# Attention without TensorE transposes: probabilities turned in 32x32 squares on VectorE, gathered inside SBUF by transfers, three of eight key blocks in native float32

## The reference, cut to what matters

```python
x = x + attention(layernorm(x), ctx, ctx, gamma)   # 8 heads, scale 1/sqrt(128), on (B, 1024, 1024)
x = x + mixture(layernorm(x))
# attention: qh = q.reshape(B, 8, 128, L), kh = vh = ctx.reshape(B, 8, 128, L), L = 1024
qk  = einsum('bhdq,bhdl->bhql', qh, kh) * scale
ret = einsum('bhql,bhdl->bhdq', softmax(qk), vh)   # times gamma
# mixture: alpha = softmax(relu(x W1 + b1) W2 + b2); out = sum_k alpha_k U_k (V_k x), 8 experts of rank 64
```

## Time and profile before

| what | value |
|---|---|
| median of three runs | 1776.61 us |
| span of the profiled execution (first to last instruction) | 1775.2 us |
| granted TensorE clock | 1.00 of full speed throughout |
| PE busy | 98% of the span |
| DVE, ACT, POOL busy | 64%, 44%, 27% |
| data moved | 159.98 MB |

### The profile page before, as it was taken

The page is one execution under the profiler, slowest core; times in us unless marked ns, Lnnn a source line. Parts: engine busy times, 40 slices in busy tenths (PEclk is TensorE's granted clock), DMA queues, the critical chain, the costliest instruction groups (busy, mean ns, idle before and its releaser), DMA issues.

```text
span 1775.2 us, 25213 instructions
## 1 busy us (share of the span) xinstructions
PE 1739.8 (98%) x8736; PEld 1394.5 (79%) x8736; DVE 1137.6 (64%) x1608; ACT 774.0 (44%) x1314; POOL 473.1 (27%) x297
## 2 busy tenths in 40 slices
PE   7999999999999999999999999999999999999999
PEld 5778787878787877878787778787877878787877
DVE  7888888898888888888889743232423333232312
ACT  5666666666666666666666431212122121212120
POOL 4444445353544444444534200000000000000000
PEclk9999999999999999999999999999999999999999
DMA  4632323332334333333333403121121203021202
GB/s 149 220 102 95 113 86 110 93 118 95 118 95 118 95 112 101 95 115 88 109 93 106 160 1 107 36 95 47 65 77 37 105 0 138 4 101 40 95 0 72
DMA packets 73389, 159.98 MB, mean 90 GB/s; under 512 B 17552, under 2 KB 17552, under 8 KB 73360
## 3 DMA queue, kind: packets, MB, share of 16 engines
q1 hardware_dynamic: 73360, 159.59, 28.1%
...
...
## 4 chain that ended last, share of the span: by engine, by line
PE 85%; DVE 11%; issue 2%; ACT 1%; DMA 0%; DVEq 0%; POOL 0%
PE scores L850 20%; PE attended L429 16%; PE scores L396 15%; PE scores L893 10%; PE turned L410 10%; PE turned L911 5%; PE attended L911 5%; DVE q L507 4%; DVE pt_lo L486 3%; PE scores L930 2%; DVE neg_max L477 2%; DVE scaled L527 2%; ACT pt_hi L343 1%; PE turned L865 1%; PE turned L868 1%
## 5 line engine op out<-in xcount | busy, mean ns | idle before, releaser
L343 ACT ACTIVATE pt_hi<-turned 128x512 fp32r<-128x512 f32 x512 | 304.7, 595 | 314.9 <-PE turned L410 314.9
L410 PE MATMUL turned<-ident,probs 128*128 128x128 f32 x2048 | 388.9, 272 | 3.3 <-ACT probs L348 2.6
L410 PEld LDWEIGHTS turned<-ident,probs 128*128 128x128 f32 x2048 | 282.7, 140 | 100.8 <-ACT probs L348 19.4
L477 DVE TENSOR_REDUCE neg_max<-scores 128x1 f32<-128x1024 f32 x256 | 312.2, 1219 | 72.5 <-PE scores L396 67.6
L486 DVE TENSOR_TENSOR pt_lo<-turned,pt_hi 128x512 fp32r<-128x512 f32 x512 | 328.9, 683 | 30.9 <-ACT pt_hi L343 20.3
L348 ACT ACTIVATE probs<-scores,neg_max 128x1024 f32<-128x1024 f32 x256 | 285.9, 1117 | 48.0 <-DVE neg_max L477 47.9
L429 PE MATMUL attended<-pt_hi,v_hi 128*128 128x512 f32 x512 | 243.9, 476 | 18.8 <-DVE scaled L527 18.8
L429 PE MATMUL attended<-pt_hi,v_lo 128*128 128x512 f32 x512 | 223.6, 437 | 0.0
L429 PE MATMUL attended<-pt_lo,v_hi 128*128 128x512 f32 x512 | 223.2, 436 | 0.0
L988 DVE TENSOR_TENSOR ht_lo<-hidden,ht_hi 128x512 fp32r<-128x512 f32 x64 | 44.3, 693 | 258.6 <-ACT ht_hi L797 258.6
L850 PE MATMUL scores<-nt_hi,w_hi 128*128 128x512 f32 x512 | 200.0, 391 | 0.0
...
## 6 DMA issues: line engine op xcount, KB each, us to landing
...
```

What stands on the lines that cost most here:

```text
L343: nc.scalar.activation(pt_hi[half][:, 4 * part:4 * part + 4, col:col + P], src[:], ACT.Copy).then_inc(s_hi, 1)
L410: ins = pe.transpose(dst[:, i % 4, :], probs[j % 2][:, i * P:(i + 1) * P], ident[:])
L477: nc.vector.tensor_reduce(neg_max[:, j:j + 1], scores[j % 2][:], AX_X, ALU.max, negate=True).then_inc(s_max, 1)
```

## The change

The probabilities are no longer transposed on TensorE. For each query block DVE turns `probs` (128x1024) in squares of 32x32 into `pb` (`blocks`), which puts each square in place but leaves squares in the wrong partitions. When the four blocks of a half are turned, SP issues 16 transfers from SBUF to SBUF (`gather`), each from 32 partitions to 32 partitions, 8 key blocks by 128 columns, 128 KB in runs of 512 B; together they fill `pt`, keys on partitions, 2 MB. ACT copies key blocks 0 to 4 into high parts (`hi`), POOL subtracts the low parts; key blocks 5 to 7 are not split: they are multiplied once, in float32, with values `v_nat` loaded as they are. The last steps of a head come ten blocks behind its scores (`LAG`). There are now two PSUM banks `attended`.

Work moves between engines: the query scaling goes from DVE to ACT (as scale and shift), the gains from DVE to ACT, the high parts of keys and values from POOL to ACT, the low parts of the probabilities from DVE to POOL. The weights W1 and V, whose place in SBUF `pb` and the first `hi` now use, are loaded behind the last gathers instead of in the first heads; the first chunk is split by ACT and DVE. The mixture's products and loop stay the same, with other PSUM banks.

```diff
...
+    SPLIT = 5
+    NAT = JB - SPLIT
+    QB = 4
+    SB = P // QB
+    LAG = 10
+    QUARTER_KEYS = ((0, 1), (1, 2), (2, 3), (3, 5))
...
-    pt_hi, pt_lo = [], []
-    for b in range(2):
-        pt_hi.append(place.tensor(f"pt_hi{b}", [P, JB, BANK], F32R))
-        pt_lo.append(place.tensor(f"pt_lo{b}", [P, JB, BANK], F32R))
+    place = SbufMap(nc, shared["loaded_at"])
+    pb = [place.tensor(f"pb{b}", [P, QB * JB, HALF, SB]) for b in range(2)]
+    hi = [[place.tensor(f"pt_hi{b}_{q}", [P, hi_k - lo_k, BANK], F32R) for q, (lo_k, hi_k) in
+           enumerate(QUARTER_KEYS)] for b in range(1)]
+    top = SbufMap(nc, shared["top_at"])
+    x1_out = [top.tensor(f"x1_out{b}", [P, BANK]) for b in range(2)]
+    hi.append([(top if q < 2 else place).tensor(f"pt_hi1_{q}", [P, hi_k - lo_k, BANK], F32R)
+               for q, (lo_k, hi_k) in enumerate(QUARTER_KEYS)])
+    assert place.at == shared["loaded_end"]
+    pt, pt_lo = [], []
+    for b in range(4):
+        under = SbufMap(nc, place.at)
+        pt.append(place.tensor(f"pt{b}", [P, JB, BANK]))
+        pt_lo.append(under.tensor(f"pt_lo{b}", [P, JB, BANK], F32R))
...
+    v_hi = [place.tensor(f"v_hi{b}", [P, SPLIT, P], F32R) for b in range(2)]
+    v_lo = [place.tensor(f"v_lo{b}", [P, SPLIT, P], F32R) for b in range(2)]
+    v_nat = [place.tensor(f"v_nat{b}", [P, NAT, P]) for b in range(2)]
...
+    def quarter_in(h, n, j, parity, lag):
+        back = (j - lag) // JB
+        at = (j - lag) % JB
+        if isinstance(h, int) and h + back < 0 or isinstance(h, int) and h + back >= heads:
+            return None
+        return n + (j - lag), at // 4, at % 4, h + back, (parity + back) % 2
...
+            sp.dma_start(v_raw[:, 0:SPLIT, :], ctx_t[rows_of(h), 0:SPLIT * P].rearrange("p (b d) -> p b d", d=P)
+                         ).then_inc(s_v_in, 16)
+        def load_v_native(h, parity):
+            sp.dma_start(v_nat[parity][:], ctx_t[rows_of(h), SPLIT * P:].rearrange("p (b d) -> p b d", d=P)
+                         ).then_inc(s_vn_in, 16)
...
+        def gather(h, n, half, parity):
+            sp.wait_ge(s_blocks, n + 4 * half + 4)
+            dst = pt[2 * parity + half]
+            for a in range(QB):
+                for g in range(QB):
+                    sp.dma_start(dst[SB * g:SB * g + SB, :, P * a:P * a + P],
+                                 pb[half][SB * a:SB * a + SB, g::QB, :, :].rearrange("p k j c -> p k (j c)")
+                                 ).then_inc(s_gather[half], 16)
+        def send_gain(h, half):
+            sp.wait_ge(s_gain, h * 2 + half + 1)
+            sp.dma_start(scratch[bass.ds(h * 2 + half, 1), :].rearrange("a (p j) -> (a p) j", p=P),
+                         gain[half][:]).then_inc(s_gain_out, 16)
+        def spread_gain(h, half):
+            sp.wait_ge(s_gain_out, (h * 2 + half) * 16 + 16)
...
+            known = isinstance(h, int)
+            more = not (known and h + 2 >= heads)
+            if not first:
+                gather(h - 1, n - JB, 1, 1 - parity)
+                send_gain(h - 1, 0)
+            if not (known and h < 2):
+                store_x1(h - 2, 0)
             if last:
                 load_first(n)
+            if more:
+                sp.wait_ge(s_klo, h + 2)
+                load_k(h + 2)
             if not first:
+                spread_gain(h - 1, 0)
+            if not (known and h < 2):
+                sp.wait_ge(s_pv, n - JB)
+            load_v_native(h, parity)
             if not last:
+                sp.wait_ge(s_vlo, h + 1)
                 load_v(h + 1)
             if not first:
+                send_gain(h - 1, 1)
+            if not (known and h < 2):
+                store_x1(h - 2, 1)
+            if not first:
+                load_residual(h - 1)
+                spread_gain(h - 1, 1)
+            gather(h, n, 0, parity)
             if more:
                 sp.wait_ge(s_q32, h + 2)
                 load_x(h + 2)
...
+        gather(h - 1, n - JB, 1, 1)
+        sp.wait_ge(s_gather[0], heads * GATHERS)
+        for tile, dram in shared["w1_low_loads"]:
+            sp.dma_start(tile, dram).then_inc(shared["s_w1_low"], 16)
+        send_gain(h - 1, 0)
+        store_x1(h - 2, 0)
+        spread_gain(h - 1, 0)
+        sp.wait_ge(s_gather[1], heads * GATHERS)
+        for k, (tile, dram) in enumerate(shared["w1_high_loads"]):
+            sp.dma_start(tile, dram).then_inc(shared["s_w1_high"][k], 16)
+        send_gain(h - 1, 1)
+        store_x1(h - 2, 1)
+        load_residual(h - 1)
+        spread_gain(h - 1, 1)
+        sp.wait_ge(s_pv, n)
+        for tile, dram in shared["v_loads"]:
+            sp.dma_start(tile, dram).then_inc(shared["s_v_all"], 16)
...
+        def low_keys(h, b):
+            pool.wait_ge(s_khi, h + 1)
+            nc.gpsimd.tensor_tensor(k_lo[b][:], k_raw[:], as_f32(k_hi[b][:]), ALU.subtract).then_inc(s_klo, 1)
+        def low_values(h, b):
+            pool.wait_ge(s_vhi, h + 1)
+            nc.gpsimd.tensor_tensor(v_lo[b][:], v_raw[:, 0:SPLIT, :], as_f32(v_hi[b][:]), ALU.subtract).then_inc(s_vlo, 1)
...
+        def low_probs(quarter):
+            if quarter is None:
+                return
+            count, half, q, _, parity = quarter
+            keys = slice(*QUARTER_KEYS[q])
+            pool.wait_ge(s_pthi, count + 1)
+            nc.gpsimd.tensor_tensor(pt_lo[2 * parity + half][:, keys, :], pt[2 * parity + half][:, keys, :],
+                                    as_f32(hi[half][q][:]), ALU.subtract).then_inc(s_ptlo, 1)
...
+            early = isinstance(h, int) and h < 2
+            for j in range(JB):
+                low_probs(quarter_in(h, n, j, parity, LAG - 1))
+                if j == 1 and not last:
+                    low_keys(h + 1, 1 - parity)
+                if j == 3:
+                    low_values(h, parity)
+                    if not early:
+                        add_residual(h - 2, 1)
+                if j == 4 and not last:
+                    scale_of_queries(h + 1, 1 - parity)
+                if j == 6 and not last:
+                    low_queries(h + 1, 1 - parity)
+                if j == 7 and not first:
+                    add_residual(h - 1, 0)
+                if last and j in (4, 6):
+                    first_factor(j // 2 - 2)
...
-        def high_probs(t, j, n, part, early):
-            s_turn, s_hi = (s_turn0, s_hi0) if part == 0 else (s_turn1, s_hi1)
-            half = j // HALF
-            act.wait_ge(s_turn, t + 1)
-            if j % HALF == 0 and not early:
-                act.wait_ge(s_pv, n - JB + 4 * half + (2 if part == 0 else 4))
-            src = turned0 if part == 0 else turned1[j % 2]
-            col = j % HALF * P
-            nc.scalar.activation(pt_hi[half][:, 4 * part:4 * part + 4, col:col + P], src[:],
-                                 ACT.Copy).then_inc(s_hi, 1)
+        def high_probs(quarter):
+            if quarter is None:
+                return
+            count, half, q, head, parity = quarter
+            if q == 0:
+                act.wait_ge(s_gather[half], head * GATHERS + GATHERS)
+            if not (isinstance(head, int) and head < 1):
+                act.wait_ge(s_pv, count - (JB - 1))
+            nc.scalar.activation(hi[half][q][:], pt[2 * parity + half][:, slice(*QUARTER_KEYS[q]), :],
+                                 ACT.Copy).then_inc(s_pthi, 1)
         def exps(s, j, b):
             act.wait_ge(s_max, s + 1)
+            if not (isinstance(s, int) and s < 2):
+                act.wait_ge(s_blocks, s - 1)
             nc.scalar.activation(probs[j % 2][:], scores[j % 2][:], ACT.Exp, bias=neg_max[:, j:j + 1],
                                  accum_out=row_sum[b][:, j:j + 1]).then_inc(s_exp, 1)
+        def queries(h, b):
+            act.wait_ge(s_qshift, h + 1)
+            if not (isinstance(h, int) and h == 0):
+                act.wait_ge(s_qlo, h)
+            nc.scalar.activation(q32[:], x_raw[:], ACT.Identity, bias=q_shift[b][:],
+                                 scale=q_scale[b][:]).then_inc(s_q32, 1)
...
+        def high_keys(h, n, b):
+            act.wait_ge(s_k_in, h * 16 + 16)
+            if not (isinstance(h, int) and h < 2):
+                act.wait_ge(s_scores, n - JB)
+            nc.scalar.activation(k_hi[b][:], k_raw[:], ACT.Copy).then_inc(s_khi, 1)
+        def high_values(h, n, b):
+            act.wait_ge(s_v_in, h * 16 + 16)
+            if not (isinstance(h, int) and h < 2):
+                act.wait_ge(s_pv, n - JB)
+            nc.scalar.activation(v_hi[b][:], v_raw[:, 0:SPLIT, :], ACT.Copy).then_inc(s_vhi, 1)
...
             for j in range(JB):
-                back = (n + j - 1, (j - 1) % JB, n if j else n - JB)
-                early = first or (j == 0 and isinstance(h, int) and h == 1)
-                if not (first and j == 0):
-                    high_probs(*back, 0, early)
                 exps(n + j, j, parity)
-                if not (first and j == 0):
-                    high_probs(*back, 1, early)
```

(85 more changed lines are left out.)

361 lines of the change are left out of this document (123 added, 238 removed).

## The result

The changed kernel takes 1882.27 us (median of four runs, 1880.05 to 1884.17) against 1776.85 (1776.59 to 1777.53): the ratio is 1.0592, 95% interval 1.0577 to 1.0607. It is slower by 5.9%, above the forecast of 1650 and above its range.

What follows compares the result with a forecast made beforehand. It took DVE (25.0 us a head), transfers (25), PE (23.2) and POOL (22.6) as likeliest bounds, giving 26.2 a head: 5.5 + 838 + 22 + 782.8 = 1648 of span, forecast 1650 us, range 1605 to 1830.

Steps and rivals of the forecast that it cites:

- SP, the step that failed: SP's queue in each head: 43 issues at 0.43 us, 18.5 us, upper end 29.7.
- Transfers, 25 a head: Transfer engines in each head: old transfers 10.3 us plus gathers 15, total 25; upper end 31.1.
- rival 1: Attention heads: transfers bound them, 32-partition gathers at half rate; 31.1 us a head, 1812 in all; chance 0.35.
- a half takes 7.5: Gathers of one half of a head: 7.5 us of transfers, hidden under 3.6 blocks (11.7 us).
- The stretch behind the heads, 22 us,: From the last exponential to the mixture's first product: 22 us, against 17 in the kernel before.
- Fits in the same 22: Behind the last gathers: loading w1's low half (5 us) and two splits (1.06, 1.2) add nothing to the 22 us.
- rival 2: DVE's square transposes in the heads take 2.32 us, making DVE the bound: 33.8 us a head, 1893; chance 0.07.
- rival 3: Native float32 products on PE cost 1.67 us: 29.0 us a head, 1740 in all; chance 0.08.
- the mixture: The part after the attention: keeps its products and loop, 782.8 us as before.
- rival 4: Attention heads: PE isn't unloaded because the transposes' replacement is late at every block; 1776; chance 0.05.
- DVE's term: DVE's work in each head: 23.8 us plus 1.2 for small operations beside POOL, 25.0.
- 1.2 for uneven blocks: Each head: 1.2 us added for uneven blocks among nearly equally busy engines, giving 26.2.

Runs made afterwards that it cites:

- e3_one_copy: The changed kernel with each half's 16 gathers made one 2 MB transfer over all 128 partitions, to wrong places; 1664.46 us.
- e10_sp_order: The changed kernel with only SP's issue order within a head changed (waits for the gain, place of x's load); 1824.09 us, ratio 1.0266 to before.
- e11: The changed kernel with 4 KB runs, gathers alternating between partition halves, and SP's new issue order; 1781.26 us, ratio 1.0036 to before.
- e12: As e11, with the gain's transfers to DRAM issued by ACT instead of SP, a semaphore for each half; 1726.28 us, ratio 0.9713 to before.
- after: The changed kernel itself, against the kernel before; 1882.27 us, ratio 1.0592.
- e1_wide: The changed kernel with gathers over all 128 partitions, still 16 issues and 512 B runs, transposition left out; 1889.24 us.
- e13_natural_order: As e12, with the 16 gathers of a half in natural instead of alternating order; 1753.27 us, ratio 0.9867 to before.

## Why the prediction was wrong, point by point

- **SP, the step that failed.** The text had 43 issues x 0.43 = 18.5, an upper end of 29.7, and left SP out of the likeliest bounds, as if it could run ahead of the others. Two parts of that fell. A gather's issue measured 0.666, near the upper end, so the 32 cost 21.3 where 32 x 0.43 = 13.8 was taken. And SP is not free: it issues in one order and its waits add to its sum. The text named load_x behind the gathers, but put no price on it, and did not count the waits for the gain's trip at all: 4.5 us a head. 21.3 + 4.2 + 4.5 + 2.6 = 32.6 is the head. e3_one_copy shows it by taking 30 issues away (26.07), e10_sp_order by moving nothing but the waits for the gain and x's load (30.83), and e11 and e12 bring it to 27.93 with the alternating order and with the gain sent from ACT.
- **Transfers, 25 a head.** After's share is 0.88 x 32.56 = 28.7 engine-us; less the old 10.3 that makes 18.4 for the gathers, between the 15 taken and the 20.8 of rival 1. "a half takes 7.5" measured 10.6 to 10.9 to issue, and the median gather lands 2.9 after its issue.
- **Rival 1** (1812, chance 0.35) had the sign, the symptoms it named (ACT's first high part and DVE's statistics waiting for a DMA) and, by way of the issue's upper end, nearly the head. Its mechanism was second: e1_wide leaves the head alone with four times the partitions, e13_natural_order prices the partitions at 0.9 us a head once SP is early. Of its signature, "a share of 1.0 at some 200 to 240 GB/s while gathers run", only the rate came true, and by luck: inside a group of gathers of after stands

```profile
608.65:619.55 10.90, 10.79 (x41) 7.48 (x40) 8.01 (x8) 5.27 (x9) 6.93 (x4) 0.97 0.82 212
```

  a rate that the issue alone comes near, 128 KB every 0.67 us being 197 GB/s. A share of 1.0 came only with e10_sp_order (1.02). Rival 1's upper bound of 1870 was passed too.
- **The stretch behind the heads, 22 us,** took 46. The rows below are from the chain of waits of after:

```profile
1051.60 3.46 DMA pt<-pb
...
1064.99 7.55 DMA gains<-gain
...
1075.76 8.53 DMA x_res<-in_x
```

  Both gathers stand in a row there (32 in 21.2 us, to 1062.9 in the timeline), the gain's 2 KB land 7.55 us after their issue with the weights of w1 ahead of them in the ring, and the residual x 8.53 us after its own. "Fits in the same 22" counted the bytes of the weights, not who queues behind them. In e12_gain_from_act the stretch is still 41 us (899.4 to 940.4), and no run tried to shorten it.
- **What held.** DVE's square transpose (1.22, measured 1.23; rival 2 falls), native float32 (0.91, measured 0.87; rival 3 falls, and the four passes of the Trainium skill's "FP8 and Floating Point Precision", TensorE Precision Notes, agree: 0.87 is 3.8 times 0.227), POOL's low parts (1.28 and 2.38) and the mixture (782.8, measured 784.8). e3_one_copy, with the gathers out of the way, has a head of 26.07 against 26.2. PE is unloaded too (rival 4 falls), 464.57 / 19.2 = 24.2 us a head there against 23.2. DVE's term was too high, 22.1 busy against 25.0: single durations were right, but the text added them up one behind the other, and their records overlap in part. So 1.2 for uneven blocks on top of 25.0 wasn't tested; over PE's 24.2 the gap is 1.9. In after PE's granted clock is 0.91 in the window and its busy time 26.5 a head; the clock was 1.00 before. What that costs wasn't tried by itself; in the windows of e3_one_copy and e12_gain_from_act, with less idle PE, it is 0.98 and 0.97.
- **Left open.** Why an SBUF-to-SBUF issue holds the queue for 0.63 us when one follows the other, and the other issues 0.37 (four loads of w1 in a row take 0.51 each, 2.04 us from 1062.91); only that neither partitions nor runs nor a partly idle ring change it. How much of the head each of the two limits takes, the issues and the narrow transfers, is not separated once the ring is full (e10 to e13). Fewer issues with the squares in their right places weren't tried.
